# Two attentions in one kernel: order of the first head's loads, where buffers are filled and zeros written, and heads beyond the last

## The chip, the cores and the metric

The kernel runs on one core of a Trainium2 chip. That core has TensorE (matmul), VectorE, ScalarE and GpSimd, a queue SyncE (SP) that issues most DMAs, and 16 DMA engines between DRAM and the on-chip memory. The metric is the device time of one execution in microseconds, the median of several; less is better.

## The reference

x is (2, 2048, 256). Two blocks follow each other, both with 16 heads of 16 features:

```
h   = layernorm(x)
q,k,v = h @ Wq.T + bq, h @ Wk.T + bk, h @ Wv.T + bv      # per head (2048, 16)
rk, rv = embK[idx], embV[idx]         # idx = clip(j - i, -64, 64) + 64
w   = softmax(q.k + q.rk)             # "relative attention"
x   = x + (w @ v + w.rv) @ Wo.T + bo

y   = layernorm(x);  h = layernorm(y) * g + b;  q,k,v = split(h @ w_qkv + b_qkv)
f   = y + softmax(q.k / 4) @ v @ w_o + b_o      # "plain attention"
x   = x + f + moe(layernorm(f))                 # 8 experts, top 2
```

With a batch of 2 each attention has 32 heads, counted t = 0 to 31, of 2048 x 2048 scores. Outside |j - i| <= 64 the relative term is one of two constants per query; inside it differs from key to key.

## The kernel before, in words

The program is a row of stages, each a block of its own in which every engine has its own instruction list and semaphores order them: the projection for the relative attention (`rel_projection`), `rel_attention`, `middle_stage` (output projection, layer norms, the second projection), `plain_attention`, a routing stage and the experts. A stage begins when all engines have left the one before.

In both attentions one head takes three kinds of work on TensorE. *Score turns* ("A", 32 a head, line 448 in the plain attention and 1084 in the relative one) multiply 128 queries by 1024 keys into one of two PSUM buffers psA; VectorE takes the maximum (lines 357, 958). They run ahead: while head t is weighed, the turns are those of head t+1 and, for the last of the 32 (12 in the plain attention, 18 in the relative one), of t+2. "M" transposes the row of maxima; SP copies it into the operand as a further row (`send_m`). *Fills* ("s", 64 banks a head in the plain attention, 68 in the relative one, lines 471 and 1124 to 1135) compute transposed scores less the maximum into three rotating banks psS; ScalarE exponentiates or copies each bank (lines 422, 1051). They run 8 and 7 banks ahead of the head's first step. *Weighing* (16 steps a head, lines 482, 1155) multiplies exps by values into psO; ScalarE evacuates it four times a head. "F" gathers a head's result at step 2 of the next head.

The order of TensorE's list is written out by hand: `body_turns`/`rel_turns` give the turns of one head, and `ORDER`, `REL_ORDER` the interleaving in each of 16 steps. `first` is the list that runs before the first body: all 32 score turns of head 0, M, and the first 12 or 18 turns of head 1. A turn waits until the turn two before it has been read (`released`). The loops are unrolled at build time.

The relative attention has more. "R" turns (four a head, steps 1 to 4, two heads ahead, line 1094) compute q.rk for 256 table columns; VectorE copies the result to rst (line 977), SP writes it to a DRAM table (`write_r`, line 741) and reads it back skewed by one column a row (`read_r`, line 747), so that each query's diagonal window stands in line; GpSimd masks it (`part_r`, line 866) into a left and a right part, dl and dr, which VectorE adds to the window's scores. For the weighing the window goes the other way: ScalarE exps it (`window_exp`, line 1055), GpSimd joins the parts (`join_p`), SP writes them skewed into a second DRAM table dr_p (`write_p`, line 751), whose other entries must be zero, and reads rows back (`read_p`, line 756), GpSimd folds (`fold_p`, line 909), TensorE transposes (bank kind "F" in `RING`: the 39th and 55th, and the last two of 68).

The places that are changed:
- In `rel_projection` GpSimd fills a tile with zeros (line 1324), and SP writes it to the table dr_p, 512 KB after each of the 8 row groups (line 1303); the stage ends when these have landed.
- At the start of each attention VectorE fills buffers: the ones of zs (lines 997, 382) and then vs, ot, ptr, ob, recb and blk (998 to 1005), or vs, ot, ob, recb (383 to 388). TensorE, ScalarE and GpSimd wait for all of them (`s_init`, `NINIT`) before their first instruction.
- SP's first DMAs of the relative attention: head 0's first half (`load_stack`, lines 718 to 726), V (`load_v`, 734 to 737), head 1's first half, head 0's second half, and then the write and read of head 0's table, alternating. In the plain attention `load_stacks` (line 268, 12 DMAs of 128 KB) follows for head 0 behind the first fill of zs, then all of V (line 310), then heads 1 and 2.
- At the end of each attention the lists go on as if there were heads 32, 33, 34: `head(t)` takes t modulo 32, so that loads, tables, score turns, maxima, 8 or 7 fills with their exps and one `lay_v` are done again for heads 0 to 2, and nothing uses them. The last thing is the gather of head 31, behind the last score turns.

## Time and profile before

| | |
|---|---|
| median of 3 runs | 4463.58 us (4450.49 to 4467.16) |
| profiled execution | 4474.94 us, of which the span from first to last instruction is 4473.2 |
| TensorE busy | 4044.6 us, 90% |
| VectorE busy | 3630.4 us, 81% |
| ScalarE busy | 3003.3 us, 67% |
| GpSimd busy | 1452.5 us, 32% |
| mean granted TensorE clock | 0.933 of full speed (2.4 GHz; the lower level is 0.5) |

The span divides into the projection (0 to 122 us), the relative attention (132 to about 2106), the middle stage (to 2272), the plain attention (2278 to about 3781), routing and experts. A row of a timeline gives the start in us, the duration, the engine (a q behind it: its queue, for DMA issues), the line, the operation, what is written <- what is read, how many instructions are merged, and in brackets the engine's idle time ahead and what ended it. The GB/s are what all DMA engines moved.

### The profile page before, as it was taken

To read this page: it belongs to the slowest core of one execution; us is meant where nothing else is said; L and a number is where in the kernel's file an instruction comes from. 1 tells how busy PE (TensorE), PEld (TensorE's weight loads), DVE (VectorE), ACT (ScalarE), POOL (GpSimd) and SP (SyncE) were. 2 spreads that over 40 slices of the span, in tenths; PEclk is the share of its full clock that TensorE was granted. 3 is DMA by queue.
4 is the path that set the end of the run, shared out by engine and by line. 5 is a ranking of instruction groups with operands and counts; after the bars stand their busy time and mean duration, and the time that the engine had idled before them with its cause. 6 is when DMAs were issued, how large, how long until landed. Compare 5 with 4: busy or idle time off the path is not lost. (4 is left out here: it accounts for less than half of the span.)

```text
span 4473.2 us, 78113 instructions
## 1 busy us (share of the span) xinstructions
PE 4044.6 (90%) x26829; PEld 2124.2 (47%) x26829; DVE 3630.4 (81%) x6524; ACT 3003.3 (67%) x5842; POOL 1452.5 (32%) x1419
## 2 busy tenths in 40 slices
PE   7599999999999999997869999999999996789997
PEld 4244444444444444444433333333333332679997
DVE  6688888888888888886778888888888886667775
ACT  3057777777777877775207888888888885256664
POOL 0156665666556656664100000000000000623322
PEclk9589999999999999998968999999999998789998
DMA  8456666666666666666662232323233232776664
GB/s 302 126 136 164 162 166 150 160 150 165 156 159 160 166 152 164 153 160 150 235 165 43 37 49 40 44 43 51 39 44 54 30 54 53 186 215 177 177 167 117
DMA packets 498921, 572.64 MB, mean 128 GB/s; under 512 B 63573, under 2 KB 438405, under 8 KB 488477
## 3 DMA queue, kind: packets, MB, share of 16 engines
q1 hardware_dynamic: 478700, 543.13, 50.6%
q0 software_dynamic: 19824, 24.52, 3.4%
q8 instruction: 213, 3.49, 0.4%
q14 instruction: 184, 1.50, 0.1%
HBM read 359.63 MB, written 210.95 MB: 128 GB/s over the span
## 5 line engine op out<-in xcount | busy, mean ns | idle before, releaser
L357 DVE TENSOR_REDUCE pa_pm<-pa_psA 128x2 f32<-128x1024 f32 x1068 | 1259.7, 1218 | 139.9 <-PE pa_psA L448 139.8
L958 DVE TENSOR_REDUCE ra_pm<-ra_psA 128x1 f32<-128x896 f32 x1074 | 1167.4, 1087 | 235.2 <-PE ra_psA L1084 223.6
L1051 ACT ACTIVATE ra_p<-ra_psS 128x512 f32<-128x512 f32 x2052 | 1093.6, 605 | 393.4 <-PE ra_psS L1124 280.1
L422 ACT ACTIVATE pa_p<-pa_psS 128x512 f32<-128x512 f32 x2054 | 1066.9, 604 | 250.6 <-PE pa_psS L471 246.3
L448 PE MATMUL pa_psA<-pa_zs,pa_qs 48*128 48x512 f32 x2136 | 830.6, 472 | 46.6 <-DVE pa_recb L388 25.9
L471 PE MATMUL pa_psS<-pa_qs,pa_zs 50*128 50x512 f32 x2056 | 798.6, 465 | 76.1 <-ACT pa_p L422 61.2
L1084 PE MATMUL ra_psA<-ra_zs,ra_qs 48*128 48x512 f32 x2148 | 781.0, 460 | 51.1 <-DVE ra_rst L977 27.8
L1124 PE MATMUL ra_psS<-ra_qs,ra_zs 50*128 50x512 f32 (+3 forms) x2183 | 724.7, 416 | 29.1 <-ACT ra_p L1051 16.1
L471 PEld LDWEIGHTS pa_psS<-pa_qs,pa_zs 50*128 50x128 f32 x2056 | 343.8, 185 | 623.0 <-ACT pa_p L422 603.5
L1155 PE MATMUL ra_psO<-ra_p,ra_vs 128*32 128x512 f32 (+3 forms) x6400 | 578.9, 468 | 0.0
L482 PE MATMUL pa_psO<-pa_p,pa_vs 128*32 128x512 f32 x4096 | 548.1, 607 | 0.0
L1124 PEld LDWEIGHTS ra_psS<-ra_qs,ra_zs 50*128 50x128 f32 x2183 | 358.6, 189 | 393.4 <-ACT ra_p L1051 297.6
L448 PEld LDWEIGHTS pa_psA<-pa_zs,pa_qs 48*128 48x128 f32 x2136 | 361.4, 189 | 221.8 <-DVE pa_pm L357 165.2
L1084 PEld LDWEIGHTS ra_psA<-ra_zs,ra_qs 48*128 48x128 f32 x2148 | 350.0, 197 | 178.1 <-DVE ra_pm L960 82.0
L336 POOL COPY pa_vs<-pa_vall 128x256 f32<-128x256 f32 x33 | 13.1, 399 | 1143.0 <-PE pa_psO L482 1067.4
L909 POOL TENSOR_TENSOR ra_blk<-ra_blk 128x508 f32<-128x508 f32 x128 | 162.9, 1272 | 478.3 <-DMA ra_blk<-window_rows 473.4
L2308 PE MATMUL mo_psH<-mo_hp,mo_w_parts 128*128 128x384 f32 x1392 | 284.8, 340 | 5.9 <-DVE mo_w_parts L2394 5.9
L2322 PE MATMUL mo_psY<-mo_w_parts,mo_hid_parts 128*128 128x256 f32 x2088 | 283.6, 281 | 0.0
L2279 POOL DMA_INDIRECT acc_rows<-mo_y,mo_ids x87 | 154.8, 1779 | 383.9 <-DVE mo_y L2449 366.2
L2322 PEld LDWEIGHTS mo_psY<-mo_w_parts,mo_hid_parts 128*128 128x128 f32 x2088 | 272.1, 189 | 4.0 <-DVE mo_hid_parts L2464 0.2
L1155 PEld LDWEIGHTS ra_psO<-ra_p,ra_vs 128*32 128x32 f32 x6400 | 198.4, 111 | 136.2 <-ACT ra_p L1051 87.2
L1055 ACT ACTIVATE ra_sw<-ra_sw,ra_nm 128x256 f32<-128x256 f32 x523 | 247.7, 526 | 0.0
(250 smaller groups left out, 5036.7 us busy)
## 6 DMA issues: line engine op xcount, KB each, us to landing
relative_rows<-ra_rst SPq DMA_DIRECT2D x136, 512.0 KB, 4.2
ra_blk<-window_rows SPq DMA_DIRECT2D x128, 512.0 KB, 4.6
mo_w_raw<-ffn_W SPq DMA_DIRECT2D x58, 1024.0 KB, 5.6
ra_zs<-k_halves SPq DMA_DIRECT2D x204, 248.0 KB, 7.3
ra_dl<-relative_rows SPq DMA_DIRECT2D x136, 256.0 KB, 5.2
window_rows<-ra_pc SPq DMA_DIRECT2D x128, 256.0 KB, 4.7
pa_qs<-q_halves SPq DMA_DIRECT2D x210, 128.0 KB, 6.4
pa_zs<-k_halves SPq DMA_DIRECT2D x210, 128.0 KB, 7.0
```

What stands on the lines that cost most here:

```text
L357: dve.reduce_max(pm[:, par, 2 * a:2 * a + 2], psA[w][:, :, :], AX.X).then_inc(s_am.h, 1)
L422: act.activation(pr[:, i % NPR, :], psS[:, slot(i), :], ACT.Exp).then_inc(s_ex.h, 1)
L448: last = pe.matmul(psA[w][:, half, :], qs[0:PR, k % U, i * P:(i + 1) * P], zs[0:PR, k % U, e * G:(e + 1) * G], start=True, stop=True)
L471: pe.matmul(psS[:, slot(i), :], zs[at:at + PR + NP2, p % U, z * P:(z + 1) * P], qs[at:at + PR + NP2, p % U, c * G:(c + 1) * G], start=True ...
L482: last = pe.matmul(psO[32 * m:32 * m + 32, :], vs[:, p % 2, 4 * (k % 4) + m, :], pr[:, (4 * k + m) % NPR, :], start=k % 4 == 0, stop=k % 4 ...
L958: dve.reduce_max(pm[:, q, i, 2 * left:2 * left + 1], psA[w][:, lo:lo + 2 * G - P], AX.X).then_inc(s_far.h, 1)
L1051: act.activation(dst, psS[:, slot(i), :], ACT.Exp if kind == "E" else ACT.Copy).then_inc(s_cp.h, 1)
L1084: last = pe.matmul(psA[w][:, half * G:(half + 1) * G], qs[0:PR, q, i * P:(i + 1) * P], zs[0:PR, q, at:at + G], start=True, stop=True)
L1124: last = pe.matmul(dst[:, lo:hi], zs[at:at + PR + NP2, q, z * P:(z + 1) * P], qs[at:at + PR + NP2, q, c * G + lo:c * G + hi], start=True, ...
L1155: last = pe.matmul(psO[32 * m:32 * m + 32, lo:hi], v[:, z, :], pr[:, (4 * k + m) % NPR, lo:hi], start=n == 0, stop=n == 3, tile_position=( ...
L2308: last = pe.matmul(psH[:, u % 3, 0:BT], w1[:, q, x, c, f * P:(f + 1) * P], hp[:, q, z, c, :], start=c == 0 and m == 0, stop=c == CH - 1 an ...
L2322: last = pe.matmul(psY[:, j, 0:D], hid[:, x, u % NHID, j * P:(j + 1) * P], w2[:, q, z, f, :], start=f == 0 and m == 0, stop=f == FC - 1 an ...
```

## The change

Buffer fills other than zs go from VectorE to GpSimd, and only work that reads these buffers waits for them. In the relative attention SP issues head 0's first half and its table's writes and reads first, then head 1, head 0's second half and V; the eight writes of zeros to dr_p come out of the projection and behind V here, with ptr as source. In the plain attention the first half of a head's load no longer waits for zs, and V comes behind head 1. Work for heads beyond 31 is left out on every engine (`real` says whether a turn belongs to a head that exists, and `released` skips those that don't).

```diff
@@ plain_attention
+        def real(t, kind, a):
+            return {"A": t + 1 + (a or 0) // 32, "M": t + 1, "F": t}[kind] < HEADS
+
         def released(engine, t, n):
-            if n < 0:
-                t, n = t - 1, n + TURNS
+            t, n = t + n // TURNS, n % TURNS
+            while not real(t, *body[n]):
+                t, n = t + (n - 2) // TURNS, (n - 2) % TURNS
...
                 for half in range(2):
+                    if half and t < U:
+                        s_one.wait(sp, t + 1)
...
             for t in range(lead):
-                s_one.wait(sp, t + 1)
                 load_stacks(t, t)
-                if t == 0:
+                if t == 1:
                     for b in range(NB):
                         sp.dma_start(vall[:, b, :, :], ...)
-            s_one.wait(sp, U)
             send_m(0, 0)
             for it in range(HEADS // U):
                 for p in range(U):
                     t = U * it + p
-                    load_stacks(t + lead, p + lead)
+                    if t + lead < HEADS:
+                        load_stacks(t + lead, p + lead)
...
-                    send_m(t + 1, p + 1)
+                    if t + 1 < HEADS:
+                        send_m(t + 1, p + 1)
@@ gpsimd
+            n = 0
+            for at, value in ((vs[:, :, :, :], 0.0), (vs[:, :, :, DK:DK + 1], 1.0), (ot[:, :, :], 1.0),
+                              (ob[:, :, :], 1.0), (recb[:, :, :], 1.0)):
+                pool.memset(at, value).then_inc(s_init.h, 1)
+                n += 1
+                s_init.wait(pool, n)
             s_vall.wait(pool, 16 * NB)
-            s_init.wait(pool, NINIT)
             lay_v(0, 0)
@@ vector
-            dve.memset(vs[:, :, :, :], 0.0).then_inc(s_init.h, 1)
...
-            dve.memset(recb[:, :, :], 1.0).then_inc(s_init.h, 1)
-            s_init.wait(dve, NINIT)
             for n, (kind, a) in enumerate(first):
...
+            s_init.wait(dve, NINIT)
...
-                        if kind == "A":
+                        if not real(t, kind, a):
+                            pass
+                        elif kind == "A":
                             reduce_turn(a, w, a_no(t, n), p + 1)
@@ scalar (exp) and tensor (fill)
+                if t == HEADS:
+                    return
@@ tensor
-            s_init.wait(pe, NINIT)
             for n, (kind, a) in enumerate(first):
...
+            s_init.wait(pe, NINIT)
             for i in range(LEAD):
                 fill(0, 0, i)
...
-                                if half == 0:
-                                    released(pe, t, n - 2)
-                                scores(body[n][1], half, w, p + 1, lambda k: it + k // U + 1)
+                                if real(t, *body[n]):
+                                    if half == 0:
+                                        released(pe, t, n - 2)
+                                    scores(body[n][1], half, w, p + 1, lambda k: it + k // U + 1)
@@ rel_attention (the same for real, released, exp, fill and score turns; also "R": t + 2)
             give_credits(sp, sems)
             load_stack(0, 0, 0, s_qa)
-            load_v(0, 0)
+            write_r(0, 0, 0)
+            write_r(0, 0, 1)
+            read_r(0, 0, 0)
+            write_r(0, 0, 2)
+            read_r(0, 0, 1)
+            write_r(0, 0, 3)
+            read_r(0, 0, 2)
+            read_r(0, 0, 3)
             load_stack(1, 1, 0, s_qa)
             s_one.wait(sp, 1)
             load_stack(0, 0, 64, s_qe)
-            for c in range(4):
-                write_r(0, 0, c)
-                read_r(0, 0, c)
+            load_v(0, 0)
+            s_init.wait(sp, 1)
+            for g in range(NG):
+                sp.dma_start(dr_p.rearrange("t (a i) q r -> (t a) i q r", a=4)[g].rearrange("i q r -> q i r"),
+                             ptr[:, 0:NT // 4 * W].rearrange("p (i r) -> p i r", r=W)).then_inc(s_zd.h, 16)
             send_m(0, 0)
...
+            s_zd.wait(sp, 16 * NG)
...
-                    write_r(t + 2, p, 0)
-                    write_r(t + 2, p, 1)
+                    if t + 2 < HEADS:
+                        write_r(t + 2, p, 0)
+                        write_r(t + 2, p, 1)
...
-                    s_am.wait(sp, 32 * (t + 2))
-                    load_stack(t + 3, p + 1, 0, s_qa)
+                    if t + 3 < HEADS:
+                        s_am.wait(sp, 32 * (t + 2))
+                        load_stack(t + 3, p + 1, 0, s_qa)
@@ gpsimd
-            s_init.wait(pool, NINIT)
+            n = 0
+            for at, value in ((ptr[:, :], 0.0), (vs[:, :, :, :], 0.0), (vs[:, :, :, DK:DK + 1], 1.0), (ot[:, :], 1.0),
+                              (blk_p[:, :, :, :], 0.0), (ob[:, :, :], 1.0), (recb[:, :, :], 1.0)):
+                pool.memset(at, value).then_inc(s_init.h, 1)
+                n += 1
+                s_init.wait(pool, n)
+            for c in range(4):
+                part_r(0, c)
             lay_v(0, 0, 1)
-            for t in range(2):
-                for c in range(4):
-                    part_r(t, c)
+            for c in range(4):
+                part_r(1, c)
...
+                    if t + 2 < HEADS:
+                        part_r(t + 2, 0)
@@ rel_projection
-            s_zero.wait(sp, 1)
...
-                sp.dma_start(tables[g].rearrange("i q r -> q i r"),
-                             zero[:, :].rearrange("p (i r) -> p i r", r=W)).then_inc(s_zd.h, 16)
...
-            s_zd.wait(sp, 16 * NG)
...
-            pool.memset(zero[:, :], 0.0).then_inc(s_zero.h, 1)
-            s_zero.wait(pool, 1)
```

## Rows read from the trace of the kernel before

**Rows 1.** Windows by stage: length; PE, PEld, DVE, ACT, POOL busy (x); granted clock, DMA.

```profile
132.00:245.00 113.00, 70.72 (x137) 32.90 (x137) 88.41 (x167) 6.74 (x14) 32.08 (x34) 0.50 0.46 102
...
2028.90:2087.00 58.10, 56.32 (x415) 28.12 (x415) 48.51 (x109) 44.15 (x88) 35.34 (x38) 0.94 0.68 158
...
2271.00:2296.50 25.50, 0.00 (x0) 0.00 (x0) 15.42 (x10) 0.00 (x0) 0.00 (x0) 0.54 0.67 127
...
2371.00:3714.20 1343.20, 1255.24 (x8163) 426.30 (x8159) 1203.49 (x1118) 1088.35 (x2095) 48.57 (x38) 1.00 0.31 43
...
3714.20:3758.70 44.50, 41.50 (x273) 14.17 (x270) 39.65 (x38) 35.95 (x70) 0.40 (x1) 1.00 0.27 37
```

**Rows 2.** SP's DMA issues in time: start us, us, line, copy; three stretches.

```profile
121.25 1.33 SPq L1303 DMA_DIRECT2D window_rows<-rel_zero  x1
...
134.07 0.61 SPq L718 DMA_DIRECT2D ra_qs<-q_halves  x1
...
152.39 0.38 SPq L741 DMA_DIRECT2D relative_rows<-ra_rst  x1
...
161.97 0.38 SPq L747 DMA_DIRECT2D ra_dl<-relative_rows  x1
...
2280.23 1.27 SPq L268 DMA_DIRECT2D pa_qs<-q_halves  x3
```

**Rows 3.** Windows of three loads or drains, columns as in rows 1; last is GB/s.

```profile
118.00:126.50 8.50, 1.82 (x9) 1.26 (x7) 2.40 (x4) 0.00 (x0) 0.00 (x0) 0.77 1.00 354
134.00:142.00 8.00, 0.00 (x0) 0.00 (x0) 7.05 (x4) 0.00 (x0) 0.00 (x0) 0.50 0.82 147
2281.00:2293.00 12.00, 0.00 (x0) 0.00 (x0) 9.72 (x7) 0.00 (x0) 0.00 (x0) 0.50 0.99 134
```

**Rows 4.** TensorE in time, at each attention's first matmul, with what ended its wait.

```profile
149.80 2.07 PE L1094 MATMUL ra_psA<-e_stack,ra_qs 48*128 48x256 f32 x8 [29.99 <-DVE ra_blk L1005]
...
2296.58 2.07 PE L448 MATMUL pa_psA<-pa_zs,pa_qs 48*128 48x512 f32 x4 [25.92 <-DVE pa_recb L388]
```

**Rows 5.** Page, DMA issues: copy, count, KB each, median us to landing.

```profile
relative_rows<-ra_rst SPq DMA_DIRECT2D x136, 512.0 KB, 4.2
...
ra_blk<-window_rows SPq DMA_DIRECT2D x128, 512.0 KB, 4.6
...
window_rows<-ra_pc SPq DMA_DIRECT2D x128, 256.0 KB, 4.7
```

**Rows 6.** GpSimd in time: one fill of the projection; first masks.

```profile
1.61 0.95 POOL L1324 MEMSET rel_zero<- 128x1024 f32 x1
...
165.08 1.26 POOL L866 TENSOR_TENSOR ra_dr<-ra_dl,masks 128x512 f32<-128x512 f32 x1 [13.21 <-DMA ra_dl<-relative_rows]
```

**Rows 7.** VectorE in time: first fill and first maximum of the relative attention.

```profile
132.11 6.67 DVE L997 MEMSET ra_zs<- 32x7936 f32 x1 [11.56 <-issue]
...
168.05 1.09 DVE L958 TENSOR_REDUCE ra_pm<-ra_psA 128x1 f32<-128x896 f32 x1 [0.43 <-POOL ra_dl L866]
```

**Rows 8.** TensorE in time, score matmuls of the last relative head.

```profile
2070.98 0.40 PE L1084 MATMUL ra_psA<-ra_zs,ra_qs 48*128 48x512 f32 x1
...
2071.22 0.62 PE L1084 MATMUL ra_psA<-ra_zs,ra_qs 48*128 48x512 f32 x2
```

**Rows 9.** Groups by line in the last relative head: shapes, count, busy us, mean ns.

```profile
L1055 ACT ACTIVATE ra_sw<-ra_sw,ra_nm 128x256 f32<-128x256 f32 x16 | 7.6, 527 | 0.0
...
L1094 PE MATMUL ra_psA<-e_stack,ra_qs 48*128 48x256 f32 x16 | 2.9, 303 | 0.1
```

**Rows 10.** Windows of the last two relative heads, columns as in rows 1.

```profile
1972.90:2001.70 28.80, 27.80 (x184) 13.25 (x183) 23.52 (x47) 18.25 (x37) 11.76 (x14) 0.88 0.73 151
2001.70:2028.90 27.20, 26.65 (x224) 13.97 (x223) 23.40 (x58) 23.86 (x50) 16.63 (x17) 1.00 0.68 182
...
2048.00:2051.00 3.00, 2.18 (x19) 1.30 (x21) 3.00 (x6) 1.81 (x4) 0.74 (x1) 1.00 1.16 321
2051.00:2058.00 7.00, 7.00 (x32) 2.98 (x24) 3.98 (x13) 3.94 (x8) 4.32 (x6) 0.51 1.02 141
```

More of the change, by code:

```diff
@@ L522, in _ @@
                                 if k == M_STEP:
-                                    released(pe, t, n - 2)
-                                    turn_m(t + 1, w)
+                                    if real(t, "M", None):
+                                        released(pe, t, n - 2)
+                                        turn_m(t + 1, w)
                                     n += 1
@@ L678, in before, with real @@
             return max(j for j in range(i - 6, i) if slot(j) == slot(i))
+        def real(t, kind, a):
+            return {"A": t + 1 + (a or 0) // 32, "R": t + 2, "M": t + 1, "F": t}[kind] < HEADS
         def released(engine, t, n):
-            if n < 0:
-                t, n = t - 1, n + RTURNS
+            t, n = t + n // RTURNS, n % RTURNS
+            while not real(t, *body[n]):
+                t, n = t + (n - 2) // RTURNS, (n - 2) % RTURNS
             kind, a = body[n]
@@ L1013, in _ @@
                     split_m(0, n % 2)
+            s_init.wait(dve, NINIT)
             for it in range(HEADS // U):
@@ L1018, in _ @@
                         w = (PT + n) % 2
-                        if kind == "A":
+                        if not real(t, kind, a):
+                            pass
+                        elif kind == "A":
                             reduce_turn(a, w, t + 1, p + 1)
@@ L1158, in weigh @@
                 last.then_inc(s_us.h, 1)
-            s_init.wait(pe, NINIT)
             for n, (kind, a) in enumerate(first):
@@ L1176, in _ @@
                     turn_m(0, n % 2, 0)
+            s_init.wait(pe, NINIT)
             for i in range(REL_LEAD):
@@ L1192, in _ @@
                             if item == "a":
-                                if half == 0:
-                                    released(pe, t, n - 2)
-                                scores(body[n][1], half, (PT + n) % 2, p + 1)
+                                if real(t, *body[n]):
+                                    if half == 0:
+                                        released(pe, t, n - 2)
+                                    scores(body[n][1], half, (PT + n) % 2, p + 1)
                                 n, half = n + half, 1 - half
@@ L1202, in _ @@
                                     w = (PT + n) % 2
+                                    if not real(t, *body[n]):
+                                        n += 1
+                                        continue
                                     released(pe, t, n - 2)
@@ L1214, in _, with rel_projection @@
             gather_heads(HEADS, PT % 2)
[L1217 removed]
+def rel_projection(nc, A, ident, sel, masks, e_stack, evc, ev_side, q2, kl2, kr2, v_rows):
     NX = 3
@@ L1261, in rel_projection @@
         vv = v_rows.rearrange("(g j p) c -> g p j c", p=P, j=TPG)
-        tables = dr_p.rearrange("t (a i) q r -> (t a) i q r", a=4)
         def column(vec, c):
```

87 lines of the change are left out of this document (45 added, 42 removed).

## The prediction

> **What bounds the kernel now.** I read the windows by stage first [rows 1]. In some 31 steady heads of the plain attention TensorE is busy 1255 of 1343 us, VectorE 1203, ScalarE 1088, at the full clock: three engines in step, with TensorE the last. The relative attention is alike: in its last head 56.3 of 58.1 us for TensorE, 48.5 for VectorE, 44.2 for ScalarE. The change leaves these steady heads alone. It works on four places where the kernel does not run like that. From 132 to 245 us TensorE is busy 70.7 of 113 us at the 1.2 GHz level (granted clock 0.50); from 2271 to 2296.5 it is not busy at all; and each attention's last head (58.1 and 44.5 us) does a whole head of scores, maxima and loads for heads that don't exist. After these I read each start instruction by instruction, and each end by groups of lines. The profiled execution took 4474.9 us (span 4473.2). That is 11.4 above the median of the timed runs, so the sum below is made as a difference and then taken from the median, 4463.6.
>
> **Part 1, zeros out of the projection.** The last of eight 512 KB writes of zeros is issued at 121.25 us, right behind the last real output [rows 2]. The DMA engines are full from 118 to 126.5 us, at 354 GB/s [rows 3], so that transfer is 524 KB / 354 = 1.5 us of the drain that the stage's end waits for. The seven earlier ones lie beside compute. Saved: 1.5 us (0.5 to 2.5; the higher end if earlier ones were in the backlog too). The eight writes come back behind the first head's tables, beside 40 us of VectorE-bound maxima; they take 8 x 1.5 = 12 us of DMA. SP has nothing due there until it sends the first head's maxima, so nothing.
>
> **Part 2, start of the relative attention.** TensorE's first instruction starts at 149.80 us, and what ended its wait is VectorE's last buffer fill (L1005) [rows 4]. The loads that it truly needs are issued from 134.07 us [rows 2]. They are 256 + 128 + 3 x 248 KB = 1.155 MB, and from 134 to 142 us the DMAs move 147 GB/s x 8 us = 1.18 MB [rows 3]; so head 0 has landed at about 142.0 us, and with the fills on GpSimd TensorE starts there. Behind it runs a chain, which now is:
> - tables on TensorE and copy on VectorE: 149.80 until the write is issued at 152.39, 2.6 us [rows 2, 4];
> - the write: 9.6 us until the read goes out at 161.97 [rows 2], because 1.2 MB of head 1, 1.2 MB of head 0's second half and all of V were issued ahead of it. The median of 136 such writes is 4.2 us [rows 5], and after the change nothing but head 0 is ahead of it;
> - the read, until GpSimd starts at 165.08: 3.1 us [rows 2, 6];
> - GpSimd's masks until VectorE's first maximum at 168.05: 3.0 us [rows 6, 7].
> After: 142.0 + 2.6 + 4.2 + 3.1 + 3.0 = 154.9, against 168.05: 13.1 us saved, 7.8 from the fills and 5.4 from the queue. From there VectorE paces the phase as before and everything shifts by that. Head 1's, V's and the second-half loads now issue after 156 us and are wanted 40 us later. Bounds: the load may land 2 us later or 1 earlier, the write may take 6 us: 9 to 15 us.
>
> Does GpSimd fill in time? The fills are 10,238 elements a partition; GpSimd filled 1024 in 0.95 us [rows 6], so 9.5 us and seven waits of about 0.2: from 132.1 to 143, before 151.9, when it must begin the masks. Were it shut out during the whole of VectorE's fill of 6.67 us [rows 7], it would be 150: still in time. That fill covers the move.
>
> The Trainium skill (GPSIMD Engine Reference, section 3.1) puts GpSimd's elementwise work at about 2.6 cycles an element of a 1.2 GHz clock. By that, an estimate, the fills would take 22.2 us and end at 154.3; the masks would start 2.4 us late, and the whole sum would be 56 instead of 58. The row of 0.95 us is a fill on this chip and decides.
>
> **Part 3, end of the relative attention.** Removed are, in the last head, 32 score turns (64 matmuls), 4 table groups, the transpose of maxima, 7 score banks of "head 32" with their copies, and 11 window exps; in the head before, 18 turns (the last ones) and 4 table groups. One score matmul shows 0.40 us and two in a row 0.62 [rows 8], so each costs TensorE 0.22 us of stream.
> - Last head, TensorE: 56.3 busy, less 64 x 0.22 = 14.1, less 2.4 (16 table matmuls, 2.9 busy with overlap), 1.5 (7 banks), 0.3 = 38.0. The clock was 0.94 over this window [rows 1], so 7.0 us at the 1.2 GHz level, 3.5 lost; if that dip goes with the tables (below), 34.5. ScalarE: 44.15, less 11 of 16 window exps (7.6 busy) 5.2, less 7 copies of 0.51 (the other 72 instructions in 36.5) 3.6 = 35.4 [rows 1, 9]. Two engines at about 35 that hand each other three banks don't run gapless; I take 38.5 and 19.6 saved. Next late is the path of the window through GpSimd and DRAM (rival B). Bounds 13 and 22.
> - Head before, first half (28.8 us, clock 0.88): 6.9 us at the lower level cost 3.5; tables 2.4; both partly: 5 saved (3 to 7). Second half (27.2 us): 36 matmuls, 7.9 us, leave TensorE, but ScalarE is busy 23.9 of 27.2 [rows 10]; 2.2 saved (0.5 to 3).
> The dip: from 2045 on the tables are made; at 2048 to 2051 TensorE is busy 2.18 of 3 us at clock 1.00, then 7 us at 0.51 [rows 10]. It waited for VectorE's table copies and maxima. Without both this wait is not there.
> Part 3: 19.6 + 5 + 2.2 = 26.8 us.
>
> **Part 4, start of the plain attention.** TensorE starts at 2296.58, released by the last fill (L388) [rows 4]. Its 12 loads of 128 KB are 1.573 MB, issued from 2280.23 behind a fill [rows 2]; from 2281 to 2293 the DMAs move 134 GB/s [rows 3], so the last lands at about 2292.7, and the first half, no longer behind the fill, goes out up to 0.5 us earlier. TensorE starts at 2292.3: 4.3 us saved (3.5 to 4.8), and not the 17 that the idle stretch suggests: the load is next late. V now goes behind head 1's load, some 12 us later, and is first wanted with the first weighing, behind 44 turns of scores.
>
> **Part 5, end of the plain attention.** Last head: TensorE 41.5 - 14.1 - 1.8 (8 banks) = 25.6; ScalarE 35.95 in 70 instructions, 0.51 each, less 6 exps of "head 32" = 32.9 [rows 1] and one weighing and evacuation after the last exp: 34, against 44.5: 10.5 saved (8 to 11). ScalarE is the bound. Head before: 12 turns leave the last six steps; a step is about 2.65 us (44.5 less two gathers of 1 us, in 16), and ScalarE fills 1088/1343 of it, 2.15, with the edges of its evacuations 2.28: 6 x 0.37 = 2.2 (1 to 3). Part 5: 12.7 us.
>
> The skipped heads' loads and GpSimd work are beside compute; the fewer credits, waits and instructions count as nothing, for the steady heads hide them.
>
> **Sum.** 1.5 + 13.1 + 26.8 + 4.3 + 12.7 = 58.4. The profiled execution would be 4474.9 - 58.4 = 4416.5, the median 4463.6 - 58.4 = 4405.2.
>
> **Rivals.**
> - A, the forecast: 4405 us. Chance 0.72.
> - B, the ends are bound by latency. In the last relative head the window goes exp, GpSimd join, write (4.7 us), read (4.6) [rows 5], fold, transpose; the last bank follows the one that frees its buffer by 12 of 68 banks, now 10 us, then 6.8, and needs about 7. If two such round trips show, the head takes 46 instead of 38.5, and the plain one 37 instead of 34: 10.5 less, 4416. For it: the two trips through DRAM are 9.3 us of latency that no engine's speed changes [rows 5]. Against: GpSimd and SP lose the tables' work that delays them. 0.13.
> - C, the starts don't come: the fills or first loads are late by the time that the 7.8 of part 2 and the 4.3 of part 4 suppose, and only the queue's 5.4 stays: 12 less, 4417. The rate of 147 GB/s in [rows 3] includes some of V, which speaks for a little of it. 0.05.
> - D, slower. With the score matmuls gone TensorE pauses for ScalarE at each bank, the granted clock falls to 0.50 and stays until the stage's end. Then TensorE is the bound: last relative head 34.5 x 2 = 69 (+11), second half of the one before (26.65 - 7.9) x 2 = 37.5 (+10), last plain head 25.6 x 2 = 51 (+7), six steps before it +3: +31 instead of -34.5, beside -18.9 of the starts and -5: 4463.6 + 31 - 24 = 4471. It decides if the lower level holds for most of these stretches (some 110 us after the change); for half of them it gives 4438. For it: the dip in [rows 10], after a stretch 73% busy. Against: 1343 us of plain heads with TensorE busy 93% and a pause at nearly every step, at 1.00 [rows 1], and that the dense weighing comes more often when the scores are gone. 0.05. The Trainium skill has this case (TensorE: Matmul & The Clock Gate, "A second HAM failure mode"): short idles between groups that cycle through PSUM banks make the clock swing. The relative heads' dips agree with it, the plain heads speak against.
> - E, little: parts 2 and 4 are taken back because the A phase is paced otherwise, and the ends by B: within 22 us of before. 0.05.
>
> **From these the numbers.** A change is told from none beyond about 0.5%, 22 us. Best ends: 2.5 + 15 + 32 + 4.8 + 14 = 68, worst ends: 0.5 + 9 + 16.5 + 3.5 + 9 = 38.5; with 6 us for a median of runs that spread over 17 us: 4389 to 4431, and up to 4438 for D's half. Faster 0.91, same 0.05, slower 0.04.
>
> **What would show it.** Right: TensorE's first work about 10 us after VectorE's first fill in the relative attention (now 17.7) and about 12.6 us behind the first load's issue in the plain one (now 16.4); the first maximum 23 us after that fill (now 36); last heads of 38 to 39 and 34 us with ScalarE at over 90%; no writes of zeros before the attention; clock 1.00 in both last heads. Wrong: TensorE waiting for GpSimd's fills; the write of the first table still over 6 us; a last relative head of 45 us whose TensorE waits for folds; clock 0.50 there. A time above 4440 would mean D or E.

## The result: 4431.8 us, and half of the forecast gain

The changed kernel runs in 4431.83 us (median of 14 runs, 4414.7 to 4451.8); the kernel before, in the same rounds, in 4459.05 (14 runs, 4436.2 to 4493.2). The ratio is 0.993, 95% interval 0.991 to 0.995: 31 us less (22 to 40); the two medians differ by 27. Twelve more runs of the changed kernel gave 4431.7 and 0.9933 (0.9909 to 0.9958). The forecast was 58.4 us less. So the change is faster, as forecast, and brings about half of what its parts were added up to.

The profiled execution took 4430.1 us (span 4428.4), 44.8 less than the profiled one of before. That is more than the runs show, and the pair must not be read as a whole: 21.7 us of it are the clock in 29 steady heads, which the change doesn't touch (below). Stage by stage, in us:

| stretch | before | after | gain | forecast |
|---|---|---|---|---|
| last output issued to first load, relative | 13.5 | 11.9 | 1.5 | 1.5 |
| first load issued to first maximum, relative | 34.0 | 21.1 | 12.9 | 13.1 |
| first maximum to transpose of head 0's maxima | 42.1 | 42.1 | 0 | 0 |
| 29 steady relative heads | 1662.3 | 1640.6 | 21.7 | 0 |
| last transpose to end of weighing, relative | 71.8 | 60.0 | 11.8 | with the next, 26.8 |
| table work out of the head before | 55.1 | 52.9 | 2.2 | |
| last matmul of the middle stage to first plain score | 25.9 | 23.8 | 2.1 | 4.3 |
| last transpose to end of weighing, plain | 54.8 | 51.6 | 3.2 | 12.7 |
| second projection of the middle stage, routing stage | 136.3, 83.2 | 139.4, 89.7 | -3.1, -6.5 | 0 |

(The 55.1 is this head at the full clock, as in the kernel starts_only below; in the profile of before it took 58.2, with 6.8 us at the lower level. What is left to the 44.8 us, in both directions, is -1.0.) The start of the relative attention in the trace of after, in time; the columns are start, duration, engine, line, operation, and in brackets the idle time with its releaser:

```profile
123.42 0.61 SPq L1352 DMA_DIRECT2D v_rows<-rel_vout  x1
135.36 0.61 SPq L738 DMA_DIRECT2D ra_qs<-q_halves  x1
...
140.67 0.95 POOL L959 MEMSET ra_recb<- 128x1024 f32 x1
...
145.09 2.07 PE L1141 MATMUL ra_psA<-e_stack,ra_qs 48*128 48x256 f32 x8 [22.43 <-DMA ra_zs<-k_halves]
...
147.60 1.51 SPq L761 DMA_DIRECT2D relative_rows<-ra_rst  x2
150.63 0.36 SPq L767 DMA_DIRECT2D ra_dl<-relative_rows  x1
153.47 1.26 POOL L904 TENSOR_TENSOR ra_dr<-ra_dl,masks 128x512 f32<-128x512 f32 x1 [11.85 <-DMA ra_dl<-relative_rows]
156.44 1.09 DVE L1007 TENSOR_REDUCE ra_pm<-ra_psA 128x1 f32<-128x896 f32 x1 [2.98 <-POOL ra_dl L904]
```

No zeros stand between the last output and the first load any more [rows 2]. TensorE's wait is ended by a load, not by VectorE's last fill [rows 4]; the write takes 3.0 us instead of 9.6. The start of the plain attention:

```profile
2231.16 1.37 SPq L275 DMA_DIRECT2D pa_qs<-q_halves  x2
...
2245.63 1.64 PE L459 MATMUL pa_psA<-pa_zs,pa_qs 48*128 48x512 f32 x3 [23.84 <-DMA pa_zs<-k_halves]
```

And windows of after, with the columns of [rows 1]: last relative head, steady plain heads, last plain head:

```profile
1987.80:2034.90 47.10, 44.40 (x352) 23.27 (x353) 3.25 (x5) 38.82 (x77) 21.45 (x22) 1.00 0.28 74
...
2309.00:3662.50 1353.50, 1265.16 (x8185) 428.76 (x8177) 1197.62 (x1112) 1092.83 (x2104) 48.55 (x38) 1.00 0.29 41
3662.50:3703.00 40.50, 36.99 (x198) 12.32 (x194) 0.69 (x1) 31.97 (x63) 0.00 (x0) 1.00 0.00 1
```

The last heads are the surprise. VectorE has nothing left to do (0.69 us where it had 39.65), a quarter of TensorE's matmuls is gone, and yet the plain one takes 40.5 us for 44.5, and the relative one 47.1 for 58.1 (of the 58.1 a part was at the lower clock, 0.94 in the mean; the other three are at the full clock) [rows 1]. In the plain one neither ScalarE (32.0 of 40.5) nor TensorE (37.0) is full.

### The profile page after: what moved, and what is told of

Its sections match the earlier page's. It is cut to its first block and busy times, and to the rows that moved or that the text cites. A ratio compares the mean times of both kernels' runs of the same rounds, so it can differ in the third digit from the quotient of the medians.

```text
span 4428.4 us, 77243 instructions
## 1 busy us (share of the span) xinstructions
PE 4001.6 (90%) x26592; PEld 2106.5 (48%) x26592; DVE 3490.8 (79%) x6304; ACT 2991.0 (68%) x5821; POOL 1445.9 (33%) x1405
## 5 line engine op out<-in xcount | busy, mean ns | idle before, releaser
L370 DVE TENSOR_REDUCE pa_pm<-pa_psA 128x2 f32<-128x1024 f32 x1024 | 1208.3, 1219 | 140.7 <-PE pa_psA L459 140.7
L1007 DVE TENSOR_REDUCE ra_pm<-ra_psA 128x1 f32<-128x896 f32 x1024 | 1113.5, 1087 | 205.9 <-PE ra_psA L1131 190.4
L433 ACT ACTIVATE pa_p<-pa_psS 128x512 f32<-128x512 f32 x2048 | 1063.5, 604 | 249.4 <-PE pa_psS L484 245.0
L484 PE MATMUL pa_psS<-pa_qs,pa_zs 50*128 50x512 f32 x2048 | 793.4, 464 | 77.3 <-ACT pa_p L433 62.8
L459 PE MATMUL pa_psA<-pa_zs,pa_qs 48*128 48x512 f32 x2048 | 797.2, 472 | 44.2 <-DMA pa_zs<-k_halves 23.8
L1131 PE MATMUL ra_psA<-ra_zs,ra_qs 48*128 48x512 f32 x2048 | 736.0, 455 | 44.9 <-DVE ra_pm L1009 23.8
L1173 PE MATMUL ra_psS<-ra_qs,ra_zs 50*128 50x512 f32 (+3 forms) x2176 | 713.8, 411 | 32.4 <-ACT ra_p L1096 17.5
L484 PEld LDWEIGHTS pa_psS<-pa_qs,pa_zs 50*128 50x128 f32 x2048 | 342.2, 185 | 626.2 <-ACT pa_p L433 606.7
L1204 PE MATMUL ra_psO<-ra_p,ra_vs 128*32 128x512 f32 (+3 forms) x6400 | 566.6, 459 | 0.0
L495 PE MATMUL pa_psO<-pa_p,pa_vs 128*32 128x512 f32 x4096 | 548.0, 607 | 0.0
L459 PEld LDWEIGHTS pa_psA<-pa_zs,pa_qs 48*128 48x128 f32 x2048 | 346.6, 189 | 214.0 <-DVE pa_pm L370 160.5
L1131 PEld LDWEIGHTS ra_psA<-ra_zs,ra_qs 48*128 48x128 f32 x2048 | 328.5, 194 | 166.4 <-DVE ra_pm L1009 85.0
L343 POOL COPY pa_vs<-pa_vall 128x256 f32<-128x256 f32 x32 | 12.7, 399 | 1057.1 <-PE pa_psO L495 1023.7
```

The lines of the kernel that those rows point to most:

```text
L370: dve.reduce_max(pm[:, par, 2 * a:2 * a + 2], psA[w][:, :, :], AX.X).then_inc(s_am.h, 1)
L433: act.activation(pr[:, i % NPR, :], psS[:, slot(i), :], ACT.Exp).then_inc(s_ex.h, 1)
L459: last = pe.matmul(psA[w][:, half, :], qs[0:PR, k % U, i * P:(i + 1) * P], zs[0:PR, k % U, e * G:(e + 1) * G], start=True, stop=True)
L484: pe.matmul(psS[:, slot(i), :], zs[at:at + PR + NP2, p % U, z * P:(z + 1) * P], qs[at:at + PR + NP2, p % U, c * G:(c + 1) * G], start=True ...
L495: last = pe.matmul(psO[32 * m:32 * m + 32, :], vs[:, p % 2, 4 * (k % 4) + m, :], pr[:, (4 * k + m) % NPR, :], start=k % 4 == 0, stop=k % 4 ...
L1007: dve.reduce_max(pm[:, q, i, 2 * left:2 * left + 1], psA[w][:, lo:lo + 2 * G - P], AX.X).then_inc(s_far.h, 1)
```

## Why a step takes 2.61 us with or without the scores

One step of the last plain head after the change, on TensorE and ScalarE (L484 fills a bank with scores for the exp L433; L495 is the weighing):

```profile
3677.12 2.06 ACT L433 ACTIVATE pa_p<-pa_psS 128x512 f32<-128x512 f32 x4 [0.54 <-PE pa_psS L484]
3677.77 0.50 PE L484 MATMUL pa_psS<-pa_qs,pa_zs 50*128 50x512 f32 x1 [0.22 <-ACT pa_p L433]
3678.20 1.07 PE L495 MATMUL pa_psO<-pa_p,pa_vs 128*32 128x512 f32 x8
3679.19 0.96 PE L484 MATMUL pa_psS<-pa_qs,pa_zs 50*128 50x512 f32 x3
3679.72 1.08 ACT L433 ACTIVATE pa_p<-pa_psS 128x512 f32<-128x512 f32 x2 [0.54 <-PE pa_psS L484]
```

Both engines wait once in each step, for each other: a loop. From the start of the exps 0.65 us until the first has ended and the next fill of its bank starts, 0.43 until the weighing behind that fill, 0.99 of weighing, 0.53 from the next fill to its exp: 2.60 us. The same steps before the change, with the next head's scores (L448) in them:

```profile
3739.20 0.40 PE L471 MATMUL pa_psS<-pa_qs,pa_zs 50*128 50x512 f32 x1
3739.20 0.40 PE L448 MATMUL pa_psA<-pa_zs,pa_qs 48*128 48x512 f32 x1
3739.39 2.06 ACT L422 ACTIVATE pa_p<-pa_psS 128x512 f32<-128x512 f32 x4 [0.54 <-PE pa_psS L471]
...
3740.05 0.49 PE L471 MATMUL pa_psS<-pa_qs,pa_zs 50*128 50x512 f32 x1 [0.20 <-ACT pa_p L422]
...
3740.47 1.07 PE L482 MATMUL pa_psO<-pa_p,pa_vs 128*32 128x512 f32 x8
```

The same waits, 0.54 and 0.20. And a score starts with the fill, at 3739.20 both, and ends with it: a matmul over partitions 0 to 47 and one over 64 to 113 run side by side. The score costs the loop nothing. The page of before had this in its list of groups, in the idle column (busy, mean ns of one, then idle time and its releaser):

```profile
L422 ACT ACTIVATE pa_p<-pa_psS 128x512 f32<-128x512 f32 x2054 | 1066.9, 604 | 250.6 <-PE pa_psS L471 246.3
...
L471 PE MATMUL pa_psS<-pa_qs,pa_zs 50*128 50x512 f32 x2056 | 798.6, 465 | 76.1 <-ACT pa_p L422 61.2
```

ScalarE waits for TensorE and TensorE for ScalarE, on the same buffer. The Trainium skill (TensorE: Matmul & The Clock Gate, "Part 3: Packing small matmuls — row/col tiling") says that matmuls whose operands lie in different row groups of the array run at the same time; the two rows at 3739.20 agree, and by that rule the scores that start with a fill would have been costed at nothing from the start.

In the relative attention most scores lie beside a fill too, but not all. One step of its last head in starts_only (below), where the scores are still done (L1124); L1170 transposes, with all 128 partitions:

```profile
2019.04 0.66 PE L1170 MATMUL ra_psS<-ident,ra_sw 128*128 128x128 f32 x4
2019.62 0.73 PE L1124 MATMUL ra_psA<-ra_zs,ra_qs 48*128 48x512 f32 x2
2020.29 0.66 PE L1170 MATMUL ra_psS<-ident,ra_sw 128*128 128x128 f32 x4
```

Two scores stand alone between the transposes and take 0.67 us. That step is 3.49 us long, and 2.77 without the scores (after); the next one, with its scores beside fills or in a wait for ScalarE, is 2.61 us in both. Of the steps of the last relative head those with transposes or table turns became shorter by 0.4 to 1.6 us each, and those of fills and scores alone by nothing, but for two (0.1 and 0.5): that is where the gain of the relative end comes from.

## The experiments

**Each half alone.** starts_only keeps the starts of the change and does the work for heads beyond the last again; ends_only is the reverse.

```diff
         def real(t, kind, a):
-            return {"A": t + 1 + (a or 0) // 32, "M": t + 1, "F": t}[kind] < HEADS
+            return True          # starts_only: in both attentions, and every other
+                                 # condition on heads beyond the last likewise
```

> The changed kernel with its ends undone: scores, maxima, tables, loads and exps for heads beyond the last are done again in both attentions; the starts (first loads first, fills on GpSimd, zeros behind the first tables) stay. Read from the pair of profiles, the starts gave 1.5 us (drain), 12.9 us (first load to first maximum) and 2.1 us (plain attention), 16.5 together: this kernel about 16 to 17 us below the one before, ratio 0.996. Last plain head as long as before (M transposes of the last real head to the last weighing 54 us), last relative one too (71 us). The forecast's own sum for this kernel was 18.9. Rival: the starts are given back in the half-clock stretches of the first heads, then ratio 0.999 or above. In the relative attention's steady heads each 6.8 us at the 1.2 GHz level should again lengthen a head of 55.1 us by about 3.1, whatever part of the change is in.

Measured: 4440.7 us (12 runs), ratio 0.997 (0.9948 to 0.9992), 14 us less; the plain end is as long as before (54.8 us), the relative one 69.4 us for 71.8, without the 6.8 us at the lower level that the profile of before has in it.

```diff
-            for at, value in ((ptr[:, :], 0.0), (vs[:, :, :, :], 0.0), ...
-                pool.memset(at, value).then_inc(s_init.h, 1)
+            dve.memset(vs[:, :, :, :], 0.0).then_inc(s_init.h, 1)
...
+            sp.dma_start(tables[g].rearrange("i q r -> q i r"), zero[:, :] ...
```

> The kernel before with only the work for heads beyond the last left out (both attentions); loads, fills and zeros as before. Theory 1 (a step is a loop of latencies: exp, score fill, weighing, score fill, exp, 2.61 us, and the next head's score matmuls lie free in it): the plain last head gives 3 us, the relative end 14, together 17: ratio 0.996. Theory 2 (the forecast: TensorE's stream of 0.22 us for each score matmul bounds the step): 39.5 us, ratio 0.991. Steps of the last plain head: 2.61 us by theory 1, 2.1 to 2.2 by theory 2.

Measured: 4439.8 us (12 runs), ratio 0.9973 (0.9958 to 0.9989), 12 to 15 us less where the forecast's view wanted 39.5. Together 25 us by the ratios and 29 by the medians: within the intervals the halves add up to the whole. In the last plain head the steps at the full clock are 2.60 to 2.70 us long; theory 2 is out. Its profile also holds what rival D feared, once:

```profile
3672.70:3695.00 22.30, 21.51 (x83) 6.85 (x82) 0.69 (x1) 13.61 (x27) 0.00 (x0) 0.70 0.00 1
```

The granted clock is 0.70 over the first half of the last plain head, 1.00 before and after it, and from the last transpose to the end are 59.3 us where after has 51.6. The same came in the profile of dve_fills (57.7), and in none of the other eight with the scores gone. The Trainium skill's "A second HAM failure mode" (TensorE: Matmul & The Clock Gate) describes such a swing behind short idles; here it comes in some executions, lasts some 20 us, and costs up to 8.

**The weighing in two pieces.** If the loop counts, a shorter piece of weighing between two fills shortens it.

```diff
-ORDER = "assaOsaas"
+ORDER = "asPsasOasa"                      # P: columns 0 to 255, O: the rest
...
+                lo, hi = part * G // 2, (part + 1) * G // 2
-                    last = pe.matmul(psO[32 * m:32 * m + 32, :], vs[:, p % 2, 4 * (k % 4) + m, :],
-                                     pr[:, (4 * k + m) % NPR, :], ...
+                    last = pe.matmul(psO[32 * m:32 * m + 32, lo:hi], vs[:, p % 2, 4 * (k % 4) + m, :],
+                                     pr[:, (4 * k + m) % NPR, lo:hi], ...
```

The places of the scores between the fills change with it, and the evacuation moves by one bank (`EVAC` 22 to 23).

> The changed kernel, with the plain attention's weighing (four matmuls of 512 columns, 1.0 us, between two fills) issued as two pieces of 256 columns, each between fills; nothing left out. Theory 1 (loop of 0.5 exp + 0.2 + 0.43 fill + 1.0 weighing + 0.54 fill to exp = 2.61 us): the loop loses 0.5 us, and the step is then set by ScalarE (2.06 for four exps and a quarter of 0.6 for the evacuation, 2.2) or VectorE (two maxima, 2.36): last plain head from 41 to 35 or 36 us, steady heads from 43.6 to 38 to 41, the kernel 80 to 150 us faster than the changed one (4280 to 4350). Theory 2 (TensorE's stream is full, 93% busy): no step shorter than 2.6, and a little slower from twice the weight loads (8 a step), 43.6 to 45 a head: 4430 to 4475.

Measured: 4524.4 us, ratio 1.0156 to the kernel before: by the medians 93 us slower than the changed kernel. Both expectations missed. In the last head, without scores:

```profile
3800.67 0.64 PE L497 MATMUL pa_psO<-pa_p,pa_vs 128*32 128x256 f32 x8
3801.24 0.73 PE L484 MATMUL pa_psS<-pa_qs,pa_zs 50*128 50x512 f32 x2
3801.90 0.64 PE L497 MATMUL pa_psO<-pa_p,pa_vs 128*32 128x256 f32 x8
```

The loop is gone (no matmul of TensorE waits), and half a step is 1.23 us: 0.57 for a piece of weighing and 0.66 for two fills, a step 2.46. That is TensorE's own stream in this form, in which two pieces cost 1.14 us and one whole weighing 1.0; from the last transpose to the end are 49.3 us for 51.6. In the steady heads a step is 2.84 (47.3 us a head, 43.6 in the changed kernel):

```profile
3739.84 0.50 PE L459 MATMUL pa_psA<-pa_zs,pa_qs 48*128 48x512 f32 x1
3739.84 0.49 PE L484 MATMUL pa_psS<-pa_qs,pa_zs 50*128 50x512 f32 x1
3740.18 0.78 PE L459 MATMUL pa_psA<-pa_zs,pa_qs 48*128 48x512 f32 x2
3740.46 0.50 PE L484 MATMUL pa_psS<-pa_qs,pa_zs 50*128 50x512 f32 x1
3740.89 0.64 PE L497 MATMUL pa_psO<-pa_p,pa_vs 128*32 128x256 f32 x8
3741.46 0.49 PE L484 MATMUL pa_psS<-pa_qs,pa_zs 50*128 50x512 f32 x1
3741.46 0.50 PE L459 MATMUL pa_psA<-pa_zs,pa_qs 48*128 48x512 f32 x1
...
3742.11 0.64 PE L497 MATMUL pa_psO<-pa_p,pa_vs 128*32 128x256 f32 x8
```

The half with one score, which starts with a fill at 3741.46, takes 1.22 us, as long as without any. The other half has three: one starts with a fill at 3739.84, one at 3740.46 (the second of the two merged in the row of 3740.18), and the one at 3740.18 stands alone. This half takes 1.62. So a score beside a fill is free, and one alone costs the step up to 0.4 us. Before, all four scores of a step started with a fill; giving that up for one of them, and 0.14 us more of weighing, cost more than the loop that it left. VectorE's maxima also follow one another with gaps of only 0.19 to 0.26 us there, so what VectorE alone would allow wasn't tested.

**Five banks for the last heads**, on top of early_loads (below). The score buffers are idle there; with five banks in rotation the fill no longer waits for the exp three banks back.

```diff
+        def bank(t, i):
+            if t < HEADS - 1 or i < LEAD:
+                return psS[:, slot(i), :]
+            x = ("x0", "x1", 2, 0, 1)[(i - LEAD) % 5]
+            return psA[w_free][:, int(x[1]), :] if isinstance(x, str) else psS[:, x, :]
...
-                s_ex.wait(pe, BANKS * t + before(i) + 1)
+                if t < HEADS - 1 or i < LEAD:
+                    s_ex.wait(pe, BANKS * t + before(i) + 1)
+                elif i >= LEAD + 2:
+                    s_ex.wait(pe, BANKS * t + i - 5 + 1)
```

> The kernel early_loads, and in the last head of each attention the score fills rotate over five PSUM banks (two of them from the score buffers, which are free there) in place of three; the weighing stays whole. Theory 1 (loop of exp, fill, weighing, fill, exp over three banks): the wait of ScalarE (0.54 us a step for TensorE) and of TensorE (0.22 to 0.32 a step for ScalarE) both go; a step of the last plain head falls from 2.61 us to TensorE's own 1.0 + 4 x 0.33 = 2.3 (or ScalarE's 2.2), the head from 41 to 36 or 37 us, the last relative head from 47 to about 42: 9 to 10 us below early_loads (4401), so 4391 to 4392. Theory 2 (TensorE's stream or the path through DRAM bounds the last heads): steps stay within 0.1 us of 2.61 and the relative last head at 47, no change. Rival D: without waits for scores the clock may fall in the last heads, as in the profile of ends_only (20 us at the 1.2 GHz level, 7.7 us lost).

Measured in the trace (L498 fills, L509 weighs, L443 exp):

```profile
3681.53 1.07 PE L509 MATMUL pa_psO<-pa_p,pa_vs 128*32 128x512 f32 x8
3682.45 1.72 ACT L443 ACTIVATE pa_p<-pa_psS 128x512 f32<-128x512 f32 x3
3682.52 0.73 PE L498 MATMUL pa_psS<-pa_qs,pa_zs 50*128 50x512 f32 x2
3683.09 0.61 PE L498 MATMUL pa_psA<-pa_qs,pa_zs 50*128 50x512 f32 x2
3683.64 1.07 PE L509 MATMUL pa_psO<-pa_p,pa_vs 128*32 128x512 f32 x8
```

From weighing to weighing 2.11 us, ScalarE without a gap. From the last transpose to the end the plain attention takes 44.3 us (51.6 with three banks) and the relative one 54.1 (60.0); 7.3 and 5.9 us less, so the last heads are 33 and 41 us long for 40.5 and 47.1. The plain one is near the 34 of the forecast and the relative one 3 us over its 38.5, for a kernel with two more banks; the expectation's 2.3 us a step was too long. It is the change of one thing, the number of banks, with no instruction more or less: the loop over three banks is shown as the cause of these 7.3 and 5.9 us. That the path through DRAM (rival B) made the relative head 47 us long is shown wrong by the same run, which leaves that path as it was; what holds the remaining 41 wasn't tested. The time of the whole, expected at 4391 to 4392, came to 4412.8, told below.

**The two halves of the relative start.** old_queue is the changed kernel with SyncE's old order, dve_fills with the fills back on VectorE; in both TensorE no longer waits for the fills. Each was run once, for its trace.

```diff
             load_stack(0, 0, 0, s_qa)
-            write_r(0, 0, 0)
...
+            load_v(0, 0)
+            load_stack(1, 1, 0, s_qa)
...
+            for c in range(4):
+                write_r(0, 0, c)
+                read_r(0, 0, c)
```

> The changed kernel with SyncE's order of the relative start as before (V, head 1 and the second half of head 0 ahead of the first tables' writes); fills stay on GpSimd. By the forecast's split: first table as early as in the changed kernel (9.7 us behind the first load's issue) and first maximum 5.4 us later than there, 26.5 us behind it (21.1 in the changed kernel, 34.0 before).

```diff
-                pool.memset(at, value).then_inc(s_init.h, 1)
+            dve.memset(ptr[:, :], 0.0).then_inc(s_init.h, 1)
+            ...                                # the same seven fills, behind zs
```

> The changed kernel with the fills of both attentions back on VectorE, in front of its first copy, but TensorE not waiting for them; SyncE's new order stays. VectorE is then busy with fills until 17.7 us behind its first one, so the first table's copy waits for them: first maximum about 7 us later than in the changed kernel; in the plain attention TensorE starts as now (14.5 us behind the first load's issue), and the first maximum up to 3 us later, since VectorE fills until 18.1 us behind its first fill.

The first read of the tables and the first maximum of old_queue:

```profile
132.20 0.61 SPq L738 DMA_DIRECT2D ra_qs<-q_halves  x1
...
150.12 0.42 SPq L761 DMA_DIRECT2D relative_rows<-ra_rst  x1
160.90 0.38 SPq L767 DMA_DIRECT2D ra_dl<-relative_rows  x1
...
167.02 1.09 DVE L1002 TENSOR_REDUCE ra_pm<-ra_psA 128x1 f32<-128x896 f32 x1 [0.40 <-POOL ra_dl L899]
```

and of dve_fills:

```profile
133.92 0.61 SPq L739 DMA_DIRECT2D ra_qs<-q_halves  x1
...
148.27 1.76 DVE L1051 MEMSET ra_blk<- 128x2048 f32 x1 [0.38 <-issue]
...
160.00 1.09 DVE L1003 TENSOR_REDUCE ra_pm<-ra_psA 128x1 f32<-128x896 f32 x1 [3.00 <-POOL ra_dl L905]
```

From the first load to the first maximum: before 34.0, GpSimd's fills with the old order 34.8 (26.5 expected), the new order with VectorE's fills 26.1 (28 expected), both 21.1. So the two are not 7.8 and 5.4 that add up. With the old order SyncE comes to the first write 17.9 us behind the first load (18.3 before), however early the table is ready, because it issues V and two more stacks first; and the write then takes 10.8 us behind their transfers. The 5 us won on TensorE are waited away there. With VectorE's fills the order brings 7.9 us, of which 6.6 are the shorter write (3.0 us for 9.6) and 1.1 that it goes out earlier (17.2 us behind the first load for 18.3), since TensorE doesn't wait for the fills; GpSimd's fills bring 5.1 once the order is there, and nothing without it. In the plain attention dve_fills has its first maximum 16.8 us behind the first load for 15.7 (up to 3 us later expected), so there the place of the fills is worth 1 us.

**Fewer bytes before the first matmul** (early_loads): separate semaphores, no load moved.

```diff
-                                         src[part, bass.ds(row, DK), bass.ds(col, S)]).then_inc(s_qz[slot].h, 16)
+                                         src[part, bass.ds(row, DK), bass.ds(col, S)]).then_inc((s_qz, s_qy)[half][slot].h, 16)
...
-                    s_qa[p % 2].wait(pe, NLD * loads)
+                    s_qa[p % 2].wait(pe, 32 * loads)
+                    if keys:
+                        s_ka[p % 2].wait(pe, 48 * loads)
```

> The changed kernel, with TensorE's first tables (relative attention) waiting for the queries alone (384 of 1155 KB) and the plain attention's first scores for the first halves of the stacks alone (786 of 1573 KB), by semaphores of their own; no load is moved. If the transfers land in the order of their issue: first table 5 us earlier (4.5 to 5 us behind the first load's issue, 9.7 now), first maximum as much, and the first plain score about 6 us earlier (8.5 us behind the first load's issue, 14.5 now); 11 us in all, 4421. Rival: the transfers share the engines and land together, then 0 to 3 us.

```profile
132.90 0.61 SPq L740 DMA_DIRECT2D ra_qs<-q_halves  x1
...
138.30 2.07 PE L1147 MATMUL ra_psA<-e_stack,ra_qs 48*128 48x256 f32 x8 [18.58 <-DMA ra_qs<-q_halves]
...
2222.26 1.46 SPq L275 DMA_DIRECT2D pa_qs<-q_halves  x3
...
2230.45 2.07 PE L460 MATMUL pa_psA<-pa_zs,pa_qs 48*128 48x512 f32 x4 [17.77 <-DMA pa_zs<-k_halves]
```

First table 5.4 us behind the first load (9.7), first maximum 17.7 (21.1), first plain score 8.2 (14.5): the transfers land in their order. The first maximum gains 3.4 us where 5 were expected. The half with 0.786 MB takes 8.2 us and the whole with 1.573 MB 14.5: 6.0 and 12.0 us at the 131 GB/s of the changed kernel's load, and 2.2 to 2.5 us around them. In time: 4401.2 us for the 4421 expected, ratio 0.9874 (0.9852 to 0.9896), and once more:

> The kernel early_loads once more, in the same rounds as banks5. Its five runs had 4396.6 to 4406.1; by the traces the starts give 13 to 14 us over the changed kernel (4431.7 in 26 runs), so about 4418; 4401 again would say that there is a gain that the traces' starts don't show.

> The changed kernel once more, in the same rounds as banks5. Its first runs had the median 4431.8 (4414.7 to 4451.8); its profile spent 6.5 us more in the routing stage (89.7 us, 82.7 to 83.8 in four other kernels) than the others. If early_loads' 30 us below it are real, this one is again 30 us above; by the starts alone (4.3 + 6.3 + 3.4 in the traces) it should be 14 us above, and the rest is the spread of half-clock stretches.

early_again took 4407.6 us (ratio 0.9904, 0.9887 to 0.9921), after_again 4431.7. Over ten runs early_loads has 4404.8, by the medians 27 us below the changed kernel. But the two never ran in the same rounds, and the kernel before had medians from 4449.9 to 4459.1 in the four sets of rounds; by the ratios to it, 0.9874 and 0.9904 for 0.993 and 0.9933, early_loads is 12 to 26 us below. The traces' starts give 10 to 13 (3.4, 6.3, and up to 3.4 in the plain attention's first head: 53.0 us between its transposes for 53.0 to 56.4). Whether there is more than that isn't shown.

> The kernel banks5 once more. In its trace the plain attention's end took 7.3 us less than in early_loads and the relative one's 5.9, but its median of six runs was 4412.8 against 4401.2 of early_loads. By the traces it should be 13 us below early_loads in the same rounds; if the half-clock stretches of the relative attention's steady heads (1772.8 us between transposes in the one profile, 1789.8 in the other) are what hides it, the two medians differ by less than their spread of some 25 us, but this one is the lower.

banks5 and banks5_again: 4412.8 and 4403.8, ratios 0.9896 and 0.9897; over twelve runs 4408.5. In the same rounds banks5_again is 3.8 us below early_again, where the traces wanted 13. This version and early_loads beat the kernel before; they lie below the changed kernel too, clear of the intervals only in early_loads' first runs. They can't be told from each other by time, although the ends of banks5 are 13 us shorter in both traces.

## What hides 13 us: the clock in the relative attention's steady heads

Windows over the same 29 relative heads, columns as in [rows 1], of the kernel before, of ends_only and of banks5_again:

```profile
294.80:1957.10 1662.30, 1603.08 (x11982) 808.73 (x11978) 1412.39 (x3148) 1280.51 (x2552) 1023.83 (x1061) 0.96 0.67 159
```

```profile
296.20:1926.60 1630.40, 1570.85 (x11981) 792.93 (x11977) 1411.68 (x3148) 1278.81 (x2552) 1027.38 (x1062) 0.98 0.68 163
```

```profile
277.40:1939.10 1661.70, 1602.72 (x11982) 808.46 (x11978) 1412.60 (x3148) 1280.54 (x2552) 1026.09 (x1063) 0.96 0.66 159
```

The same instructions, the same busy time of VectorE and ScalarE, and 32 us of difference. A head takes 55.1 us at the full clock and 58.2 where 6.8 us of it are granted at the 1.2 GHz level. Before and banks5_again have 143 us of such stretches in these heads, ends_only 65; over the twelve profiles a line through the lengths is 1606 us + 0.39 for each us at the lower level (65 to 143). Neither the change nor its parts can be seen to set it: the kernels with the old ends have 119 and 143, those with the new ones 65 to 143. early_loads had 75 and 89, banks5 119 and 143, and is 19 us longer in these heads in the mean, which takes back more than its 13 us. Whether the runs of the two differ so by chance wasn't shown.

## Right and wrong, by the prediction's steps

- **Part 1, 1.5 us:** right. 13.5 us from the last output to the first load in the two kernels that write zeros there, 11.9 in six of the ten others, and 12.4 in the four with early_loads' semaphores.
- **Part 2, 13.1:** right in sum, 12.9. The load took 9.7 us instead of 7.9, since the sum had the bytes alone and nothing around them; the write 3.0 instead of 4.2, and that these two misses nearly cancel was luck. Its split into 7.8 for the fills and 5.4 for the queue was wrong: without the order of the queue the fills bring nothing. GpSimd's fills ran from 132.00 to 141.62; a fill of 1024 elements took 0.95 us, as in [rows 6], and so VectorE's own fill beside them cost nothing. The 22.2 us worked out from the Trainium skill (GPSIMD Engine Reference, section 3.1) did not come: that section gives the 2.6 cycles for an operation with two inputs, and a fill has none.
- **Part 3, 26.8:** mis-sized, 11.6 (2.2 in the head before, by its 55.1 us at the full clock, and 9.4 in the last, by starts_only's undisturbed 69.4 us; 11.8 against the profile of before with its dip). The steps that failed: "each costs TensorE 0.22 us of stream", and the last head's 38.5 from 38.0 and 35.4 us of busy engines. Measured, these are 44.4 and 38.8 us busy, and the head is as long as neither: its sixteen steps take 2.6 us, those of the loop over three banks, or up to 3.3, since it has four fills and the window's transposes more than the plain head, and 4.3 in the one with the gather; they make 47.1. The sentence "two engines at about 35 that hand each other three banks don't run gapless" had the cause in it and gave it 3 us instead of 12. The two dips that the forecast wanted to win back: in the head before, only the profile of before has one. The other is gone in starts_only, where the score matmuls and tables are still done; so it goes and comes with that work in place. And all ten profiles without the work have a new one of 6.8 us right behind the last transpose (in after from 1978.8 to 1985.7, mean clock 0.51). It lies in the 60.0 us and, at 0.39 us for each us at the lower level (an estimate from the steady heads), costs 2.7 of them.
- **Part 4, 4.3:** 2.1 in the pair. The load stands behind the fills, as forecast, but takes 14.5 us from its issue and not 12.1: the 2.2 to 2.5 us around the bytes were not in the sum.
- **Part 5, 12.7:** 3.2. ScalarE's 32.9 us of work was right (32.0), the step was not shortened at all. "Head before 2.2" was zero: the steps without scores are as long as the others.
- **Rivals:** B's 46 us for the last relative head was near the measured 47.1 and wrong in its mechanism; D occurs, but in two of ten profiles and for about 20 us. The 4431.8 lies just above 4431, the end of the range worked out from the parts, and inside only because the range reached out to 4438 for the half of D, which did not happen: luck, and not because a loss of this kind had been thought of.
- **The signs:** the first maximum came 22.7 us after VectorE's first fill (23 forecast), and the clock was 1.00 in both last heads. But the last heads were 47.1 and 40.5 us long with ScalarE at 82 and 79% (38 to 39, 34 and over 90% forecast). Of the signs of being wrong one came, a last relative head of over 45 us; but in it TensorE's matmuls wait for ScalarE, 11 times and 2.6 us together, and never for the folds.

Measured sum: 1.5 + 12.9 + 11.6 + 2.1 + 3.2 = 31.3 us, against 31 by the ratio of the runs and 27 by their medians. So close an agreement is more than one profile of each kernel can promise.

## What to carry to other kernels

An engine that is busy 93% of a stage doesn't show that its instructions are the bound: look in the list of groups for two lines that wait for each other on one buffer. There the step is a loop of latencies, and only what lies in the loop (a shorter piece in it, one more buffer) is worth anything; before an instruction is costed, look whether it starts at the same time as another, or stands alone. And where two causes of delay stand one behind the other in a queue, remove each alone before giving either a price.

## What the runs showed of the hardware

- Two matmuls over partitions 0 to 47 and 64 to 113 start and end together (3739.20, 0.40 us both); four weighing matmuls of 32 columns each start within 0.02 us of each other. Two matmuls over partitions 0 to 47 between transposes over all 128 stand alone and take 0.67 us (2019.62 in starts_only).
- The granted clock of one engine moved a part of the kernel with fixed instructions by 32 us, 0.7% of the whole and as much as this change: kernels within that of each other need a comparison by stages, or many runs.
- GpSimd filled 2048 elements a partition in 1.80 us and VectorE in 1.76, at the same time in different buffers.
